# A conditioned residual kernel in fp32: new engine orders in its first two pairs, one copy and one split moved in every pair

## The chip, the cores and the metric

The kernel runs on one core of a Trainium2 chip. The metric is the device time of one execution in microseconds. Inside the core TensorE (PE) multiplies, VectorE (DVE), ScalarE (ACT) and GpSimd (POOL) work on whole tiles, and SyncE (SP) issues most DMAs. Each engine runs its own list of instructions in order and waits on semaphores that the others raise. PE has two clock levels, 1.2 and 2.4 GHz; the profile shows the granted clock as a share of the higher.

## The reference

```
B, C, T = 64, 128, 1024
w = cond_weights[conditions]                       # (64, 128, 128)
x = x + einsum('bct,bcd->bdt', x, w)               # residual 1, over channels
H = einsum('btd,od->bto', x, W)                    # W is 1024 x 1024
xa = einsum('btd,brd->btr', x, A[adapter])         # rank 16, 8 adapters
delta = einsum('btr,bor->bto', xa, Bm[adapter]) * scalings[adapter]
x = x + H + delta                                  # residual 2
```

The kernel swaps the two linear maps: it first multiplies the raw x by W plus identity (with the adapter columns riding along), and then by the batch's own 128 x 128 matrix plus identity.

## The kernel before, in words

The 64 batches are done in 32 pairs. The contraction over 1024 columns of x is cut into four blocks of 256, the 1024 columns of W into three of 342 (the last is shorter in truth), so a pair is 2 x 4 times a 4 x 3 grid of weight blocks, b00 to b32. From the second pair (pair 1) on, it isn't multiplied densely: 20 products of sums of x with sums of weight blocks (numbered 0 to 19, function `multiply`) give the two batches' results together. The sums of x (u, u12, u67, u910, u11, u54, u3) and the raw blocks (a001, a02, a03, a1, a13) are made for each pair, the 20 sums of weights once. Every operand is split in two halves of the fast fp32r type: ACT copies the high half (`hi_...`), DVE subtracts it to get the low half (`rest_...`), and PE does three matmuls, hi x hi, hi x lo, lo x hi. For the weights the same is done by `hi_of` and `rest_of`, and `in_place` is that for a sum that stands where its low half is kept.

Pair 0 has no split weights yet. PE multiplies it densely in full fp32 (`dense`, twelve blocks in the order of the table DENSE) while DVE and POOL make the sums of weights, each in the order of a table (DVE_SUMS, POOL_SUMS), and ACT and DVE split them (SPLITS). POOL adds the identity into blocks (`add_identity`, sums named i21a and so on) and scales the adapter's columns (`first_rides` for pair 0, `make_rides` and `rest_rides` for later ones).

After the products of a pair come its adapter part and its condition part. The xa columns are split on DVE (`split_xa`, `rest_xa`, batch 0 and batch 1 apart), PE turns them (`turn0`, `turn1`), ACT copies the turned ones to g_sb (`turned_xa`), and PE multiplies them with b_stack (`lora`), which holds the adapter's second factor in halves. It comes from b_split, a table in device memory that the kernel writes at its start from b_raw (halves made in z_hi and z_lo of batch 0). The results are split again (z_hi, z_lo) and multiplied by c_hi and c_lo (`condition`, into o_ps0 and o_ps1); ACT evacuates them into o_sb (`evacuate`), and SP stores o_sb, batch 1 first and then batch 0 through the same buffer, so that the evacuation of batch 0 waits for the store of batch 1 (semaphore stored).

`step(i, j)` on each engine is the list for one pair. `run_steps` loops over pairs 2 to 29 and then writes two more steps. Pairs 0 and 1 have lists written out by hand on ACT, DVE and PE, with the work of the weights among them; SP and POOL have their own starts. In the list of pair p on ACT and DVE stands also the making of x for pair p + 1. Waits are written by `after` (a semaphore counted in pairs) and `made` (a sum of weights). Lines of the trace are those of the helpers: L475 is every ACT copy, L826 every DVE subtraction and L829 every addition, L1089 DVE's sums of weights, L1260 a product, L1406 a dense block, L1275 `lora`, L1287 and L1280 the turns, L1296 to L1298 the condition product.

Of the kernel before, what the change touches and what calls it, by code (L numbers as in the profile page):

```python
# [4 lines left out]
P = 128  # L5
# [3 lines left out]
def cond_resid_kernel(nc, xT, cond_idx, adapter_idx, cond_w, wB, lora_a, lora_b, scalings, out):  # L9
    f32 = mybir.dt.float32  # L10
# [44 lines left out]
    DENSE = ("b12", "b01", "b30", "b21", "b20", "b10", "b00", "b11", "b31", "b02", "b32", "b22")  # L55
    SPLITS = ("17", "13", "15", "5", "2", "0", "4", "14", "18", "10", "7", "11", "9", "8", "16", "1", "3", "19", "6", "12")
    POOL_SUMS = ("i21a", "i21b", "i10", "i00", "i11a", "i11b", "i32", "i22")
    DVE_SUMS = ("s", "v", "5", "f", "2", "e", "0", "4", "14", "18", "y", "10", "7", "11a", "11", "9", "12a", "16a",
                "1a", "16", "6", "1", "3", "19a", "12", "19")

    with ExitStack() as ctx:
# [235 lines left out]

        @block.sync
        def _(sp):
# [41 lines left out]
            def load_w(b):  # L341
                k, j = int(b[1]), int(b[2])
                sp.dma_start(w_block(b), wB[k, j, :, :, :]).then_inc(w_landed[b], 16)  # L343

# [19 lines left out]

            load_x(0, 0, 0, 0)
            load_w("b12")
            load_x(0, 0, 0, 1)
            load_w("b01")
            load_w("b30")
            sp.dma_start(s_tab[:, :], scalings.to_broadcast([P, NAD])).then_inc(s_landed, 16)  # L370
            sp.wait_ge(adapter_landed, 16)
            load_a(0, 0, 0)
            load_w("b21")
            load_w("b20")
            sp.dma_start(b_raw[:, :], lora_b.rearrange("a r o -> (a r) o")).then_inc(b_raw_landed, 16)
            for b in ARRIVAL[5:]:
                load_w(b)
# [10 lines left out]
            sp.wait_ge(b_lo_ready, 1)  # L388
            for a in range(NAD):
                sp.dma_start(b_split[a, 1, :, :], z_lo[0][a * R:(a + 1) * R, :].bitcast(f32)).then_inc(b_saved, 16)  # L390
            sp.wait_ge(b_saved, 32 * NAD)
            load_b(0, 0, 0)
            step(0, 0)
            step(0, 1)
# [8 lines left out]
        def _(pool):  # L403
# [42 lines left out]
            pick_scalings(0, 0, 0)  # L446
            pool.wait_ge(a_landed, 32)
            pool.wait_ge(s_picked, 2)
            first_rides("b30")
            pool.wait_ge(w_landed["b21"], 16)  # L450
            add_identity("b21", 0, 170, 0, 128)
            add_identity("b21", 1, 298, 0, 44)
            first_rides("b20")
            first_rides("b10")
            first_rides("b00")
            pool.wait_ge(w_landed["b10"], 16)
# [3 lines left out]
            pool.wait_ge(w_landed["b11"], 16)  # L460
            add_identity("b11", 0, 0, 86, 42)
            add_identity("b11", 1, 42, 0, 128)
# [10 lines left out]
        def _(act):  # L473
# [121 lines left out]
            def hi_z00(i, j, d):  # L595
                after(act, lora_done["00"], i, j, d)
                after(act, o_done[0][0], i, j, d - 1)
                if exists(i, j, d) and not exists(i, j, d - 1):
                    act.wait_ge(b_saved, 32 * NAD)
                copy(z_hi[0][:, 0:N], main_of(bank_of(j, d, "alpha"))).then_inc(z_hi_ready["00"], 1)  # L600
# [43 lines left out]
            def step(i, j):  # L644
# [59 lines left out]

            act.dma_start(adapter_sb[:, :], adapter_idx).then_inc(adapter_landed, 16)
            act.wait_ge(ident_ready, 1)
# [4 lines left out]
            hi_of("13", slot("hi", "19"))  # L711
            made(act, "v")
            in_place("15")
            made(act, "5")
            in_place("5")
# [19 lines left out]
            hi_a02(0, 0, 1)  # L735
            dense_through(act, "b30", "b10", "b00", "b20")
            hi_rides(0, 0, 1)
            hi_u(0, 0, 1)
            hi_of_c(0, 0)
            hi_u910(0, 0, 1)  # L740
            turned_xa(0, 0, 0, 1)
            hi_u11(0, 0, 1)
            turned_xa(0, 0, 0, 0)
            made(act, "10")
            in_place("10")
            whole_block("10", c10_sb, "pi10")
            whole_block("11", c11_sb, "pi11")
            hi_z10(0, 0, 0)
            hi_z11(0, 0, 0)
            made(act, "7")  # L750
            in_place("7")
            made(act, "11", "e")
# [4 lines left out]
            made(act, "9", "f")  # L757
            in_place("9")
# [4 lines left out]
            whole_block("02", c02_sb, "pi02")  # L763
            begin_c10(0, 1)
            hi_z02(0, 1, -1)
            evacuate(0, 1, -1, 1, 0)
            hi_u54(0, 1, 0)
            seed_pi11(0, 1)
            evacuate(0, 1, -1, 1, 1)
            made(act, "10", "1a", "16a")  # L770
            in_place("8")
            begin_c11(0, 1)
            seed_pi10(0, 1)
            made(act, "6", "16")
# [22 lines left out]
            evacuate(0, 1, -1, 0, 1)  # L797
# [26 lines left out]
        def _(dve):  # L824
# [205 lines left out]
            def step(i, j):  # L1030
# [450 lines left out]
```

## Time and profile before

| | |
|---|---|
| timed runs | 807.81 us median of 3 (806.87 to 807.81) |
| the profiled execution | 805.12 us, of it a span of 803.2 us |
| PE busy | 768.1 us (96%) |
| DVE, ACT, POOL busy | 619.6, 510.9, 190.2 us |
| mean granted clock | 0.987 |

The span is what the trace shows from the first to the last instruction. From about 100 us on the trace repeats itself once a pair, and PE waits only once more, 2.2 us at the end. The first 100 us, in which the weights arrive and are summed and split, look different: in the 40 slices of the page PE has 6, 7, 8, 5, 7 tenths where it later has 9. A timeline row gives the start, the time of the row, the engine and line, the operation and its tiles, and in brackets how long the engine had been idle and what ended that.

### The profile page before, as it was taken

How to read it: one execution, taken by the hardware profiler on the slowest of the kernel's cores; microseconds unless marked ns; L12 is line 12 of the kernel's file. 1: busy time of each engine (PE TensorE's matmuls, PEld its weight loads, DVE VectorE, ACT ScalarE, POOL GpSimd, SP SyncE). 2: the span in 40 equal slices, each digit the busy share in tenths (PEclk: the TensorE clock that was granted, in tenths of full speed). 3: DMA queues.
4: the chain of work that ended last, by engine and by line, in shares of the span. 5: the costliest groups of instructions: out<-in, count | busy, mean ns of one | idle time of the engine just before them, and what ended most of it. 6: DMA issues, size and time to landing. Idle time of an engine off the chain costs nothing.

```text
span 803.2 us, 16853 instructions
## 1 busy us (share of the span) xinstructions
PE 768.1 (96%) x4456; PEld 728.4 (91%) x4456; DVE 619.6 (77%) x1397; ACT 510.9 (64%) x1186; POOL 190.2 (24%) x428
## 2 busy tenths in 40 slices
PE   6785799999999999999999999999999999999997
PEld 4464799999999999999999999999999999999996
DVE  5695977787887778788777878877787887777764
ACT  3364566667766666676666677666666766666663
POOL 4430221222222122222211222221122222112200
PEclk9998899999999999999999999999999999999999
DMA  8522134344323443432344343233434323343221
GB/s 294 145 93 86 59 120 138 129 132 144 102 101 120 134 137 124 144 108 97 122 131 144 118 144 115 95 123 125 142 118 144 126 90 125 119 140 118 86 87 78
DMA packets 47380, 98.26 MB, mean 122 GB/s; under 512 B 6788, under 2 KB 26244, under 8 KB 47364
## 3 DMA queue, kind: packets, MB, share of 16 engines
q1 hardware_dynamic: 47362, 98.08, 37.0%
q8 instruction: 6, 0.10, 0.1%
q14 instruction: 10, 0.08, 0.0%
q10 hardware_dynamic: 2, 0.00, 0.0%
HBM read 63.45 MB, written 34.60 MB: 122 GB/s over the span
## 4 chain that ended last, share of the span: by engine, by line
PE 87%; DVE 5%; SPq 3%; DMA 2%; issue 1%; ACT 1%; ACTq 0%; DVEq 0%
PE bank L1260 72%; PE o_ps L1296 4%; PE o_ps L1297 4%; PE o_ps L1298 3%; PE bank L1275 3%; DVE w_lo_raw L1089 1%; DVE w_lo L826 1%; SPq L343 1%; DMA cond_sb<-cond_idx 1%; DMA out<-o_sb 1%; DVE x_lo L826 1%; DVE z_lo L826 1%; SPq L387 0%; DVE c_sb L829 0%; PE bank L1280 0%
## 5 line engine op out<-in xcount | busy, mean ns | idle before, releaser
L1260 PE MATMUL bank<-w_hi,x_hi 128*128 128x342 f32 (+1 forms) x1240 | 404.4, 326 | 6.7 <-ACT c_sb L475 3.5
L1260 PE MATMUL bank<-w_lo,x_hi 128*128 128x342 f32 (+1 forms) x1240 | 400.8, 323 | 0.0
L1260 PE MATMUL bank<-w_hi,x_lo 128*128 128x342 f32 (+1 forms) x1240 | 400.5, 323 | 0.0
L1260 PEld LDWEIGHTS bank<-w_hi,x_hi 128*128 128x128 f32 x1240 | 234.5, 189 | 14.4 <-ACT c_sb L475 4.3
L1260 PEld LDWEIGHTS bank<-w_lo,x_hi 128*128 128x128 f32 x1240 | 234.1, 189 | 3.6
L1260 PEld LDWEIGHTS bank<-w_hi,x_lo 128*128 128x128 f32 x1240 | 234.6, 189 | 0.0
L826 DVE TENSOR_TENSOR x_lo<-x_raw,x_hi 128x256 fp32r<-128x256 f32 (+1 forms) x279 | 150.6, 548 | 34.7 <-ACT x_hi L475 29.4
L475 ACT ACTIVATE x_hi<-x_raw 128x256 fp32r<-128x256 f32 (+1 forms) x279 | 138.1, 507 | 57.2 <-PE bank L1260 51.0
L292 POOL TENSOR_TENSOR w_lo<-a_ride,w_hi 128x160 fp32r<-128x160 f32 x31 | 16.0, 518 | 539.6 <-ACT w_hi L475 539.6
L475 ACT ACTIVATE c_sb<-bank 128x342 f32<-128x342 f32 x190 | 85.4, 451 | 39.7 <-PE bank L1260 39.0
L475 ACT ACTIVATE o_sb<-o_ps 128x512 f32<-128x512 f32 x124 | 74.0, 597 | 36.6 <-PE o_ps L1298 26.2
L475 ACT ACTIVATE z_hi<-c_sb 128x340 fp32r<-128x340 f32 (+1 forms) x128 | 60.4, 490 | 54.5 <-DVE c_sb L829 54.5
L829 DVE TENSOR_TENSOR c_sb<-bank,c_sb 128x342 f32<-128x342 f32 x186 | 91.1, 504 | 3.8 <-PE bank L1275 2.6
L826 DVE TENSOR_TENSOR x_lo<-t_sb,x_hi 128x512 fp32r<-128x512 f32 x62 | 42.9, 691 | 41.0 <-ACT x_hi L475 41.0
L826 DVE TENSOR_TENSOR z_lo<-c_sb,z_hi 128x340 fp32r<-128x340 f32 (+1 forms) x128 | 69.2, 542 | 1.3 <-ACT z_hi L475 1.3
L1296 PE MATMUL o_ps<-z_hi,c_hi 128*128 128x512 f32 x126 | 53.3, 423 | 9.7 <-ACT g_sb L475 9.7
L826 DVE TENSOR_TENSOR xa_sum<-bank,c_sb 128x16 f32<-128x16 f32 x31 | 5.4, 174 | 65.3 <-PE bank L1260 65.3
L475 ACT ACTIVATE bank<-bank 128x342 f32<-128x342 f32 (+1 forms) x93 | 41.2, 443 | 15.8 <-PE bank L1260 15.8
L1297 PE MATMUL o_ps<-z_lo,c_hi 128*128 128x512 f32 x126 | 50.3, 399 | 0.0
L1298 PE MATMUL o_ps<-z_hi,c_lo 128*128 128x512 f32 x126 | 49.9, 396 | 0.0
L1275 PE MATMUL bank<-b_stack,g_sb 128*128 128x340 f32 (+1 forms) x192 | 45.9, 321 | 2.5 <-ACT g_sb L475 2.5
L268 POOL TENSOR_TENSOR a_ride<-a_now,s_now 128x32 f32<-128x32 f32 x93 | 43.3, 490 | 18.4 <-DMA a_now<-lora_a 11.7
(85 smaller groups left out, 846.9 us busy)
## 6 DMA issues: line engine op xcount, KB each, us to landing
x_raw<-xT SPq DMA_DIRECT2D x64, 512.0 KB, 4.6
out<-o_sb SPq DMA_DIRECT2D x62, 512.0 KB, 2.6
b_stack_raw<-b_split SPq DMA_DIRECT2D x128, 128.0 KB, 2.5
a_now<-lora_a SPq DMA_DIRECT2D x64, 64.0 KB, 3.3
c_raw<-cond_w SPq DMA_DIRECT2D x64, 64.0 KB, 1.8
w_lo_raw<-wB SPq DMA_DIRECT2D x7, 342.0 KB, 7.1
w_hi_raw<-wB SPq DMA_DIRECT2D x5, 342.0 KB, 6.4
out<-x_raw SPq DMA_DIRECT2D x4, 256.0 KB, 2.0
```

The lines of the kernel that those rows point to most:

```text
L268: unit.tensor_tensor(to, a_now[:, n, k:k + count, :], s_now[:, n:n + 1].unsqueeze(2).to_broadcast([P, count, 2 * R]), ALU.mult).then_inc(a ...
L292: unit.tensor_tensor(left_rides(w_lo), rides(0, 5), left_rides(w_hi), ALU.subtract).then_inc(ride_ready, 1)
L343: sp.dma_start(w_block(b), wB[k, j, :, :, :]).then_inc(w_landed[b], 16)
L475: return nc.scalar.activation(to, x, ACT.Copy)
L826: return nc.vector.tensor_tensor(to, x, y, ALU.subtract)
L829: return nc.vector.tensor_tensor(to, x, y, ALU.add)
L1089: nc.vector.tensor_tensor(to, x, y, op).then_inc(dve_summed, 1)
L1260: last = nc.tensor.matmul(bank[:, lo:hi], x[:, left, c * C:(c + 1) * C], w[:, c, FIRST[o]:FIRST[o] + WIDTH[o]], start=opens and c == 0 and ...
L1275: nc.tensor.matmul(main_of(bank_of(j, d, role), cols.stop - cols.start), g_sb[n][:, :], b_stack[:, cols], start=False, stop=True, skip_gro ...
L1296: nc.tensor.matmul(bank[:, :], c_hi[:, n, :], z_hi[n][:, cols], start=True, stop=False)
L1297: nc.tensor.matmul(bank[:, :], c_hi[:, n, :], z_lo[n][:, cols], start=False, stop=False)
L1298: nc.tensor.matmul(bank[:, :], c_lo[:, n, :], z_hi[n][:, cols], start=False, stop=True)\
```

## The change

Pair 0 and pair 1 get other lists; two things also change in `step`, which all later pairs run.

- In `step` of ACT the copy of batch 1's turned columns (`turned_xa(i, j, 0, 1)`) goes ahead of the evacuation of batch 0's first half. In `step` of DVE the split of batch 0's columns and its rest stand next to each other and ahead of the u11 rest.
- SP's start: b12 comes first; b01 and the scalings are issued from ACT's queue; b11 comes ahead of b_raw. b_split is written by two DMAs of 512 KB instead of sixteen of 64 KB, and they stand ahead of the small loads of adapters and conditions.
- SP's list of pair 1: the two stores of pair 0's outputs come first, pair 3's x after them.
- POOL adds the identity to b21 before it scales columns, and to b11 before b10 and b00.
- PE takes the dense b21 before b30, and both turns only after the dense b31 and b02; b32 goes ahead of the first `lora`.
- ACT and DVE have other hand-written orders in pair 0 and pair 1 (ACT takes b_stack much later in pair 0; DVE makes e, 18 and y earlier).

```
@@ step of ACT
                 begin_c02(i, j)
+                turned_xa(i, j, 0, 1)
                 if exists(i, j, -1):
                     evacuate(i, j, -1, 0, 0)
-                turned_xa(i, j, 0, 1)
@@ step of DVE
                 sum_c11(i, j)
+                split_xa0(i, j)
                 if exists(i, j, 1):
                     rest_u11(i, j, 1)
-                split_xa0(i, j)
+                rest_xa0(i, j)
                 rest_z("10", i, j, 0)
-                rest_xa0(i, j)
@@ SP, its start and pair 1
+            def save_b(part, z):
+                sp.dma_start(b_split[:, part, :, :], z[:, :].bitcast(f32)).then_inc(b_saved, 16)
+            load_w(sp, "b12")
             load_x(0, 0, 0, 0)
-            load_w("b12")
             load_x(0, 0, 0, 1)
-            load_w("b01")
...
+            sp.wait_ge(b_hi_ready, 1)
+            save_b(0, z_hi[0])
+            sp.wait_ge(b_lo_ready, 1)
+            save_b(1, z_lo[0])
             sp.wait_ge(first_scaled, 8)
             load_a(0, 0, 1)
             sp.wait_ge(cond_landed, 16)
             load_c(0, 0, 0)
-            sp.wait_ge(b_hi_ready, 1)
-            for a in range(NAD):
-                sp.dma_start(b_split[a, 0, :, :], z_hi[0][a * R:(a + 1) * R, :].bitcast(f32)).then_inc(b_saved, 16)
...
             step(0, 0)
-            step(0, 1)
+            load_b(0, 1, 0)
+            store(0, 1, -1, 1)
+            load_a(0, 1, 2)
+            store(0, 1, -1, 0)
+            after(sp, lo_ready["u54"], 0, 1, 0)
...
+            load_x(0, 1, 2, 0)
+            load_x(0, 1, 2, 1)
+            load_c(0, 1, 1)
@@ PE, pair 0
             dense("b12")
             dense("b01")
+            made(pe, "i21b")
+            dense("b21")
             pe.wait_ge(first_scaled, 2)
             dense("b30")
...
+            dense("b31")
+            dense("b02")
             pe.wait_ge(ident_r_ready, 1)
             turn1(0, 0)
             turn0(0, 0)
-            dense("b31")
-            dense("b02")
+            made(pe, "i32")
+            dense("b32")
@@ ACT, pair 0
             in_place("18")
+            hi_a001(0, 0, 1)
+            hi_a03(0, 0, 1)
             hi_u12(0, 0, 1)
-            hi_a001(0, 0, 1)
-            take_b(0, 0)
-            hi_a03(0, 0, 1)
...
             hi_u11(0, 0, 1)
-            turned_xa(0, 0, 0, 0)
+            take_b(0, 0)
             made(act, "10")
             in_place("10")
+            turned_xa(0, 0, 0, 1)
+            turned_xa(0, 0, 0, 0)
@@ DVE, pair 0
             rest_of("17", w_block("b12"))
             add("s", slot("hi", "19"), w_block("b12"), w_block("b01"), ALU.subtract)
+            rest_of("13", slot("hi", "19"))
             dve.wait_ge(w_landed["b30"], 16)
```

ACT in pair 0, from the copies of x for pair 1 to the first adapter results. b_stack is the adapter's second factor, a_ride the scaled adapter columns, g_sb the turned columns. Before:

```order
L475 ACTIVATE x_hi<-t_sb 128x512
L475 ACTIVATE x_hi<-x_raw1 128x512
L475 ACTIVATE b_stack<-b_stack_raw 128x1024
L475 ACTIVATE x_hi<-x_raw1 128x256
L475 ACTIVATE x_hi<-x_raw1 128x512
L475 ACTIVATE x_hi<-x_raw1 128x256
L475 ACTIVATE w_hi<-a_ride 128x5x2x16
L475 ACTIVATE w_hi<-a_ride 128x4x2x16
L475 ACTIVATE x_hi<-u_sb 128x256
```

And now:

```order
L484 ACTIVATE x_hi<-u_sb 128x256
L484 ACTIVATE w_hi<-a_ride 128x5x2x16
L484 ACTIVATE w_hi<-a_ride 128x4x2x16
L484 ACTIVATE c_hi<-c_raw 128x256
L484 ACTIVATE x_hi<-t_sb 128x512
L484 ACTIVATE x_hi<-x_raw1 128x256
L484 ACTIVATE b_stack<-b_stack_raw 128x1024
L484 ACTIVATE w_hi<-w_lo_raw 128x2x342
L484 ACTIVATE g_sb1<-o_ps1 128x128
```

The copy of b_stack has moved from ahead of six copies (three of x, two of the rides, one of u) to behind all of them and those of c, u910 and u11 too.

SP in the list of pair 1, before, behind the loads into b_stack_raw (x_raw1 is the buffer of the odd pairs, out<-o_sb a store):

```order
L323 DMA b_stack_raw<-b_split 32x1024 x2
L303 DMA x_raw1<-xT 128x1024 x2
L339 DMA out<-o_sb 128x1024
L308 TENSOR_LOAD adapter_sb
L308 ISA x2
```

And now:

```order
L327 DMA b_stack_raw<-b_split 32x1024 x2
L343 DMA out<-o_sb 128x1024
L312 TENSOR_LOAD adapter_sb
L312 ISA x2
...
L318 DMA a_now<-lora_a 128x128
L343 DMA out<-o_sb 128x1024
L307 DMA x_raw1<-xT 128x1024 x2
```

The first store has moved ahead of the loads of x, and the loads of x behind both stores.

ACT in pair 1, around the copy of batch 1's turned columns, before:

```order
L475 ACTIVATE o_sb<-o_ps0 128x512
L475 ACTIVATE g_sb1<-o_ps1 128x128
L475 ACTIVATE w_hi<-w_lo_raw 128x2x342 x3
L475 ACTIVATE x_hi<-t_sb 128x512
L475 ACTIVATE o_sb<-o_ps1 128x512
```

And now:

```order
L484 ACTIVATE o_sb<-o_ps0 128x512
L484 ACTIVATE g_sb1<-o_ps1 128x128
L484 ACTIVATE o_sb<-o_ps1 128x512
L484 ACTIVATE w_hi<-w_lo_raw 128x2x342 x3
L484 ACTIVATE x_hi<-t_sb 128x512
```

The evacuation of o_ps1 has moved ahead of the last three weight splits (19, 6, 12) and a copy of x.

## Rows read from the trace of the kernel before

**Rows 1.** Windows: stretch, its length, busy time by engine, clock, DMA share, GB/s.

```profile
100.00:123.36 23.36, 23.36 (x142) 22.60 (x141) 18.11 (x43) 15.30 (x37) 5.31 (x13) 1.00 0.37 125
```

**Rows 2.** Waits of PE in the first 100 us: total, times, longest.

```profile
PE o_ps L1296 <- ACT g_sb L475: 9.7, 1, 9.7
```

**Rows 3.** Waits of DVE in the first 100 us, the small early ones.

```profile
DVE w_lo_raw L1089 <- POOL w_lo_raw L429: 1.2, 1, 1.2
...
DVE w_hi_raw L1089 <- POOL w_hi_raw L429: 0.7, 1, 0.7
DVE w_hi_raw L1089 <- DMA w_hi_raw<-wB: 0.5, 1, 0.5
DVE z_lo L826 <- ACT z_hi L475: 0.4, 1, 0.4
```

**Rows 4.** Timeline of DVE, its start and the instructions behind its long waits.

```profile
7.66 0.87 DVE L826 TENSOR_TENSOR w_lo<-w_lo_raw,w_hi 128x684 fp32r<-128x684 f32 x1 [5.89 <-ACT w_hi L475]
...
40.76 0.52 DVE L826 TENSOR_TENSOR x_lo<-u_sb,x_hi 128x256 fp32r<-128x256 f32 x1 [7.28 <-ACT x_hi L475]
...
78.93 0.87 DVE L826 TENSOR_TENSOR w_lo<-w_lo_raw,w_hi 128x684 fp32r<-128x684 f32 x1 [8.03 <-ACT w_hi L475]
...
88.25 0.43 DVE L826 TENSOR_TENSOR x_lo<-x_raw,x_hi 128x256 fp32r<-128x256 f32 x1 [0.74 <-ACT x_hi L475]
```

**Rows 5.** Timeline of PE: turn, two dense blocks, product 17 twice, one slow matmul.

```profile
32.57 0.44 PE L1287 MATMUL o_ps<-ident_r,xa_cols 128*128 128x128 f32 x1 [3.92 <-DVE xa_cols L826]
...
33.02 6.29 PE L1406 MATMUL bank<-w_lo_raw,x_raw 128*128 128x342 f32 x16
...
48.38 0.58 PE L1260 MATMUL bank<-w_hi,x_hi 128*128 128x342 f32 x1
...
80.33 0.50 PE L1260 MATMUL bank<-w_hi,x_lo 128*128 128x358 f32 x1
...
88.74 0.42 PE L1260 MATMUL bank<-w_hi,x_hi 128*128 128x342 f32 x1 [1.64 <-DVE x_lo L826]
```

**Rows 6.** Timeline of ACT: b_raw, b_stack, the evacuation of pair 0, three weight splits.

```profile
14.91 1.06 ACT L475 ACTIVATE z_hi<-b_raw 128x1024 fp32r<-128x1024 f32 x1 [2.49 <-DMA b_raw<-lora_b]
...
37.81 1.06 ACT L475 ACTIVATE b_stack<-b_stack_raw 128x1024 fp32r<-128x1024 f32 x1 [8.51 <-DMA b_stack_raw<-b_split]
...
77.47 0.60 ACT L475 ACTIVATE o_sb<-o_ps 128x512 f32<-128x512 f32 x1 [10.35 <-DMA out<-o_sb]
...
78.12 2.10 ACT L475 ACTIVATE w_hi<-w_lo_raw 128x684 fp32r<-128x684 f32 x3
```

**Rows 7.** Timeline of SP's queue: saves, loads from b_split, the first store.

```profile
23.01 3.67 SPq L387 DMA_DIRECT2D b_split<-z_hi  x8
26.72 3.65 SPq L390 DMA_DIRECT2D b_split<-z_lo  x8
33.64 1.77 SPq L323 DMA_DIRECT2D b_stack_raw<-b_split  x4
...
71.30 0.38 SPq L339 DMA_DIRECT2D out<-o_sb  x1
```

**Rows 8.** Windows while large loads and while small saves run, columns as in rows 1.

```profile
18.00:20.00 2.00, 2.00 (x8) 1.27 (x8) 1.79 (x3) 0.91 (x2) 2.00 (x3) 1.00 1.08 381
...
26.00:28.00 2.00, 2.00 (x9) 1.30 (x8) 2.00 (x3) 0.77 (x1) 1.92 (x3) 1.00 0.73 135
```

**Rows 9.** Timeline of POOL, the first and the last row of pair 1's rides.

```profile
24.46 2.18 POOL L268 TENSOR_TENSOR a_ride<-a_now,s_now 128x32 f32<-128x32 f32 x3 [0.31 <-DMA a_now<-lora_a]
...
29.98 0.31 POOL L288 TENSOR_TENSOR a_ride<-a_now,a_ride 128x32 f32<-128x32 f32 x1
```

**Rows 10.** Timeline of a steady pair: ACT's g_sb copy, DVE's u11 rest, product 17.

```profile
133.74 0.27 ACT L475 ACTIVATE g_sb<-o_ps 128x128 fp32r<-128x128 f32 x1
...
137.97 0.42 DVE L826 TENSOR_TENSOR x_lo<-x_raw,x_hi 128x256 fp32r<-128x256 f32 x1
...
140.28 0.32 PE L1260 MATMUL bank<-w_hi,x_hi 128*128 128x342 f32 x1
```

More of the change, by code:

```diff
@@ L53, in cond_resid_kernel @@
     ARRIVAL = ("b12", "b01", "b30", "b21", "b20", "b11", "b10", "b00", "b32", "b31", "b02", "b22")
[L55 to L58, printed above, removed]
+    DENSE = ("b12", "b01", "b21", "b30", "b20", "b10", "b00", "b11", "b31", "b02", "b32", "b22")
+    SPLITS = ("17", "13", "5", "15", "2", "0", "4", "14", "18", "10", "7", "11", "9", "8", "16", "1", "3", "19", "6", "12")
+    POOL_SUMS = ("i21a", "i21b", "i11a", "i11b", "i10", "i00", "i32", "i22")
+    DVE_SUMS = ("s", "5", "v", "f", "e", "2", "0", "18", "4", "y", "14", "10", "7", "11a", "11", "12a", "9", "16a",
                 "1a", "16", "6", "1", "3", "19a", "12", "19")
@@ L363, in step @@
                     load_c(i, j, 1)
+            def save_b(part, z):
+                sp.dma_start(b_split[:, part, :, :], z[:, :].bitcast(f32)).then_inc(b_saved, 16)
+            load_w(sp, "b12")
             load_x(0, 0, 0, 0)
-            load_w("b12")
             load_x(0, 0, 0, 1)
-            load_w("b01")
-            load_w("b30")
-            sp.dma_start(s_tab[:, :], scalings.to_broadcast([P, NAD])).then_inc(s_landed, 16)
+            load_w(sp, "b30")
+            load_w(sp, "b21")
             sp.wait_ge(adapter_landed, 16)
             load_a(0, 0, 0)
-            load_w("b21")
-            load_w("b20")
+            load_w(sp, "b20")
+            load_w(sp, "b11")
             sp.dma_start(b_raw[:, :], lora_b.rearrange("a r o -> (a r) o")).then_inc(b_raw_landed, 16)
-            for b in ARRIVAL[5:]:
-                load_w(b)
+            for b in ARRIVAL[6:]:
+                load_w(sp, b)
             sp.dma_start(cond_sb[:, :], cond_idx).then_inc(cond_landed, 16)
@@ L384, in _ @@
             load_c(0, 0, 0)
-            sp.wait_ge(b_hi_ready, 1)
-            for a in range(NAD):
-                sp.dma_start(b_split[a, 0, :, :], z_hi[0][a * R:(a + 1) * R, :].bitcast(f32)).then_inc(b_saved, 16)
[L388 to L391, printed above, removed]
+            sp.wait_ge(b_saved, 32)
             load_b(0, 0, 0)
             step(0, 0)
-            step(0, 1)
+            load_b(0, 1, 0)
[3 more added lines that the diff above has]
+            after(sp, lo_ready["u54"], 0, 1, 0)
+            after(sp, lo_ready["a02"], 0, 1, 0)
+            after(sp, lo_ready["u3"], 0, 1, 0)
+            load_x(0, 1, 2, 0)
+            load_x(0, 1, 2, 1)
+            load_c(0, 1, 1)
             run_steps(sp, step)
@@ L446, in _ @@
             pick_scalings(0, 0, 0)
+            pool.wait_ge(w_landed["b21"], 16)
+            add_identity("b21", 0, 170, 0, 128)
+            add_identity("b21", 1, 298, 0, 44)
             pool.wait_ge(a_landed, 32)
@@ L455, in _ @@
             first_rides("b00")
+            pool.wait_ge(w_landed["b11"], 16)
+            add_identity("b11", 0, 0, 86, 42)
+            add_identity("b11", 1, 42, 0, 128)
             pool.wait_ge(w_landed["b10"], 16)
@@ L703, in in_place @@
                 hi_of(o, slot("lo", o))
+            load_w(act, "b01")
             act.dma_start(adapter_sb[:, :], adapter_idx).then_inc(adapter_landed, 16)
+            act.dma_start(s_tab[:, :], scalings.to_broadcast([P, NAD])).then_inc(s_landed, 16)
             act.wait_ge(ident_ready, 1)
@@ L711, in _ @@
             hi_of("13", slot("hi", "19"))
+            made(act, "5")
+            in_place("5")
             made(act, "v")
             in_place("15")
-            made(act, "5")
-            in_place("5")
             act.wait_ge(b_raw_landed, 16)
@@ L1145, in _ @@
             first_rest(0)
+            add_identity_c(0, 0)
             sum_u910(0, 0, 1)
[L1147 removed]
             rest_u(0, 0, 1)
             sum_u11(0, 0, 1)
+            rest_c(0, 0)
             rest_u910(0, 0, 1)
[L1151 removed]
             rest_u11(0, 0, 1)
[L1153 to L1155 removed]
             made(dve, "y")
             add("10", slot("lo", "10"), slot("hi", "6"), slot("lo", "8"), ALU.subtract)
+            in_place("18")
             rest_u67(0, 0, 1)
@@ L1222, in _ @@
             rest_xa0(0, 1)
+            sum_u67(0, 1, 1)
+            rest_u12(0, 1, 1)
             sum_u910(0, 1, 1)
@@ L1413, in _ @@
             dense("b01")
+            made(pe, "i21b")
+            dense("b21")
             pe.wait_ge(first_scaled, 2)
             dense("b30")
-            made(pe, "i21b")
-            dense("b21")
-            pe.wait_ge(first_scaled, 8)
+            pe.wait_ge(first_scaled, 4)
             dense("b20")
+            pe.wait_ge(first_scaled, 6)
             made(pe, "i10")
             dense("b10")
+            pe.wait_ge(first_scaled, 8)
             made(pe, "i00")
@@ L1435, in _ @@
             lora("12", 0, 0, 0)
-            made(pe, "i32")
-            dense("b32")
             made(pe, "i22")
```

100 lines of the change are left out of this document (44 added, 56 removed).

## The prediction, made before the changed kernel ran

> **What bounds the kernel now.** I first took the windows. Once the pairs run at their regular pace, PE is busy for the whole of its window: 23.36 us of 23.36 at clock 1.00, beside 18.11 on DVE and 15.30 on ACT [rows 1]. Orders on ACT or DVE can gain nothing there. What there is to win lies in the first 100 us, so I read the waits of that stretch. PE stood still 9.7 us for a copy into g_sb [rows 2]. DVE has four small waits of 1.2, 0.7, 0.5 and 0.4, together 2.8 us [rows 3], and three that its timeline shows.
>
> Which engine carries the first 90 us? Take the single stalls of DVE: it starts at 7.66, stands 7.28 us before 40.76, runs without a break from there until 70.90, stands 8.03 us before 78.93, and 0.74 us before 88.25 [rows 4]. That last instruction makes the low half of u11, and PE's product 17 of pair 2 waits for it and starts at 88.74 [rows 5]. So the first 88.74 us are the work of DVE plus its stalls, and PE has room in them. From product 17 of pair 2 on, order and work are nearly the same in both kernels and soon PE is full. The gain is therefore what is taken off DVE's ledger up to that product.
>
> The causes of the two large stalls are on other engines. At 37.81 ACT has stood 8.51 us for b_stack_raw, with the copies that DVE needs (u, u910, c) queued behind it; at 77.47 it has stood 10.35 us for an output store, with the weight splits 19, 6 and 12 behind it [rows 6]. The first goes back to SP: sixteen 64 KB saves of b_split, issued from 23.01 to 30.37, and only then the loads from it at 33.64. The second: the store of pair 0's batch 1 is issued at 71.30, since SP first waits for the low half of a02 and issues pair 3's x; ACT goes on 6.2 us later [rows 6, 7].
>
> **The change part by part.** I keep DVE's ledger, with the durations of the trace.
>
> (1) Start. b12 now goes first and b01 beside it from ACT's queue. Before, x of batch 0 (512 KB) and b12 (342 KB) were ahead of DVE's first split. Now it is b12 with up to 342 KB of b01: 170 to 512 KB less, at 381 GB/s [rows 8] 0.45 to 1.35 us earlier. I take the middle, **+0.9**. PE pays for it: x of batch 0 is behind 342 KB more, so PE starts 0.9 us later. That is free, since PE has slack until the pair 1 products. The row shows the DMA engines at a share of 1.08, with no capacity to spare. The Trainium skill ("DMA: Bandwidth & Descriptors", section "Issuing engines are not separate DMA queues") says that DMAs started from different engines run on the same 16 engines and interleave, and that a second queue saves only issue time; by that the term is 0.45, and the total 0.45 less. It speaks against this part, not against the rest.
>
> (2) Early waits. The old four small ones, 2.8 us, go or are replaced. New: the split of 13 stands directly behind the sum s and has to wait for ACT's copy of s, 0.1 plus 0.78, say 0.9. b_raw is now behind b11 too (342 KB more); ACT got it at 14.91 [rows 6], now at about 15.85; with 1.06 for the copy, z_lo can start at 16.9. DVE, with seven 684-element instructions at 0.78 to 0.9 more behind it, gets there at about 15.7: 1.2. The sum f has its identity block earlier, since POOL does b21 first. b30 has as many bytes ahead of it as before, so about 0.1. Net **+2.8 - 2.2 = +0.6**.
>
> (3) The stall of 7.28. Two saves of 512 KB replace sixteen issues (7.36 us of SP's queue), and they go ahead of the adapter loads. ACT now takes b_stack after all the copies for pair 1. But the saves lie in the queue behind x of pair 1 and ahead of the small loads. All loads end near 24.0 (3.5 MB after b_raw's 14.9 at about 385 GB/s); 1.05 MB of saves at 381 GB/s takes 2.7 us more, so b_split is saved and a_now is there at about 27. POOL's rides take from 24.46 to 30.29, 5.83 us [rows 9], so now they end at 32.9. ACT copies their high halves (0.5) and those of c (0.3) before the u910 copy; DVE gets to the rest of c at about 33.4, finds it ready at 33.75, and has to wait for u910 once more. I put 0.7 on this new wait. The loads from b_split are issued at 28.7 and land at about 33, ahead of the copy of b_stack that ACT reaches at 34.6, and PE wants the lora products at 37. Net **+7.28 - 0.7 = +6.6**. Its ends: a wait of 0 (+7.3), and the saves at the 135 GB/s of the old ones, 7.8 us instead of 2.7, which puts 5.1 us more on the rides (+1.5). I take the high rate, because the slow one belongs to a queue with a 64 KB issue every 0.46 us. The Trainium skill's same page ("Anatomy of one DMA") has about 2 us plus bytes over 436 GB/s for a DMA (a fit of another issue path), and so 3.2 us for one of 512 KB; by that a save would be down before x is, the wait would be 0 and the total 0.7 more. The old chain, one small transfer after another at 135 GB/s, agrees that issue and not bytes held it.
>
> (4) The turns on PE move behind two dense blocks, 16 matmuls that took 6.29 us partly at the lower clock [rows 5] (4.8 at the higher). The 3.92 us of PE's wait ahead of the turns is gone, and it costs nothing: DVE's columns are ready at 31, the turns come at 34.7. PE gets to product 17 of pair 1 at about 40 instead of 48.4, DVE is 8.1 earlier there, so the two stay in step. A new stop on PE: ACT's u54 copy and three others stand ahead of the seed of pi11, which makes product 0 wait 1 to 2 us. DVE doesn't hang on it.
>
> (5) The stall of 8.03. SP now issues the store when both halves of batch 1 are out, near 49.7, and even with the 6.2 us of the old one it lands at 56; ACT wants the buffer at about 59. The evacuation and the copy to g_sb run at once, and PE's second condition product isn't held. What is late next: the split of 19 needs ACT's copy, now behind the evacuation of the second half. PE's turn ends near 59.4, product 16 takes six steps of 0.16 [rows 10], 0.95; the condition product, of wider matmuls, 0.7; the evacuation 0.6 and the split 0.77 or less [rows 6]: 62.4. DVE arrives at 63.2. So **+8.0**, with 0.8 us to spare. Pair 3's x and pair 2's c are issued later now (x near 62), but they are first needed past 80.
>
> (6) Orders of the steady pairs. ACT copies g_sb before an evacuation; DVE's two short column instructions come together, ahead of the u11 rest. ACT: the g_sb copy is 0.27 long, and the evacuation slips by about 0.35 [rows 10]. DVE: the u11 rest of 0.42, started at 137.97, slips by up to 0.33, and product 17 starts at 140.28: 1.9 us of cover. **0**. At the tail PE waits on neither.
>
> Sum: 0.9 + 0.6 + 6.6 + 8.0 = **16.1 us**. Against the profiled execution: 805.12 - 16.1 = 789.0, span 803.2 - 16.1 = 787.1. The three timed runs have a median of 807.81, 2.7 above the profiled one; I carry the gain over to them: 807.81 - 16.1 = **791.7 us**.
>
> **Rivals.** *The small loads pile up behind the saves.* The saves run at the old 135 GB/s and the rides end 5.1 us later. For it: there is 1 MB in front of them that wasn't there. Against: the engines moved 381 GB/s as long as they had large transfers [rows 8]. Gain 16.1 - 5.1 = 11.0: **796.8**.
>
> *PE falls to its lower clock in pair 1.* With DVE the bound, PE gets several short stops from 58 to 73 (about 0.7, 0.9, 0.6, 1.5, 3). At 1.2 GHz a matmul takes 0.50 instead of 0.32 [rows 5, 10], and one starts every 0.30 instead of 0.16. The nine between the turn and the split of 19 and what hangs on them then take 1.4 more, of which 0.8 is spare; with a longer low stretch in pair 2 I put 2 us on it: **793.7**.
>
> *Fewer new waits.* The 2.2 and 0.7 don't come, and the start gives its upper end of 0.45 more: gain 19.5, **788.3**.
>
> *The steady orders cost every pair.* If the 0.35 on ACT and 0.33 on DVE weren't covered, each of 29 pairs would grow by 0.68: 19.7 us, more than the gain, 807.8 - 16.1 + 19.7 = **811.4**, slower than before. It decides from 0.56 us a pair (16.1 / 29). Against it: the 1.9 us of cover.
>
> *The store isn't early.* If it were held by the loads ahead of it on SP and landed after 59 + 8, the second stall would stay: **799.7**. Against it: nothing that it waits for ends after 50.
>
> **How the numbers follow.** Forecast 0.60; lower clock 0.15; pile-up 0.10; fewer waits 0.07; store not early 0.03; no gain by some collision unseen 0.02; steady cost 0.03. The range reaches from just above the case of fewest waits to just past the pile-up: 789.0 to 797.5. The measurement tells 0.2% (1.6 us) from no change. Faster 0.95, same 0.02, slower 0.03.
>
> **What would show it.** On DVE: no stall of over 2 us between 20 and 60, and none of 8 near 62; the low half of u11 at about 72. On ACT: no wait for b_stack_raw over 1 us and none for the store. On SP: the store issued near 50, before pair 3's x. On PE: product 17 of pair 1 near 40, of pair 2 near 72.6; waits in pair 1 that point at DVE; windows of 23.36 us as before. It is wrong if the small waits of DVE before 35 sum to over 4 us, if the copy of 19 is behind DVE, or if a steady window grows.

## The result, and the profile after

| | before | after |
|---|---|---|
| timed runs, median | 807.79 us of 4 (806.87 to 807.81) | 783.69 us of 4 (783.24 to 784.22) |
| ratio | | 0.9705, 95% interval 0.9688 to 0.9721 |
| the profiled execution | 805.12, span 803.2 | 783.24, span 781.3 |
| mean clock | 0.987 | 0.993 |

The change takes 24.1 us off, or 21.9 in the spans of the two profiled executions. I had said 16.1 and a range of 789.0 to 797.5: the sign was right, the size was too small, and the time lies outside the range.

The part that I had worked out came as forecast. The timeline of DVE in the kernel after, with its start and what answers to [rows 4] (the same columns):

```profile
6.53 0.87 DVE L837 TENSOR_TENSOR w_lo<-w_lo_raw,w_hi 128x684 fp32r<-128x684 f32 x1 [4.76 <-ACT w_hi L484]
...
9.03 0.87 DVE L837 TENSOR_TENSOR w_lo<-w_hi_raw,w_hi 128x684 fp32r<-128x684 f32 x1 [0.84 <-ACT w_hi L484]
...
33.95 0.53 DVE L837 TENSOR_TENSOR c_lo<-c_raw,c_hi 128x256 fp32r<-128x256 f32 x1 [0.36 <-ACT c_hi L484]
...
62.99 0.86 DVE L837 TENSOR_TENSOR w_lo<-w_lo_raw,w_hi 128x684 fp32r<-128x684 f32 x1
...
72.06 0.43 DVE L837 TENSOR_TENSOR x_lo<-x_raw,x_hi 128x256 fp32r<-128x256 f32 x1 [0.74 <-ACT x_hi L484]
```

DVE starts 1.13 us earlier than at 7.66, both long stalls are gone (the split of 19 at 62.99 waits for nothing), and the low half of u11 starts at 72.06 instead of 88.25. The causes on the other engines, to be held beside [rows 6, 7], SP's queue first and then ACT:

```profile
15.99 0.73 SPq L366 DMA_DIRECT2D b_split<-z_hi  x1
17.48 0.64 SPq L366 DMA_DIRECT2D b_split<-z_lo  x1
...
29.14 1.80 SPq L327 DMA_DIRECT2D b_stack_raw<-b_split  x4
...
49.35 0.37 SPq L343 DMA_DIRECT2D out<-o_sb  x1
```

```profile
34.65 1.04 ACT L484 ACTIVATE b_stack<-b_stack_raw 128x1024 fp32r<-128x1024 f32 x1
...
58.82 0.59 ACT L484 ACTIVATE o_sb<-o_ps 128x512 f32<-128x512 f32 x1
```

ACT waits neither for b_stack_raw nor for the store any more: neither row has a bracket. And PE (timeline), the first dense block, then product 17 of pair 1 and of pair 2:

```profile
7.48 4.90 PE L1418 MATMUL bank<-w_lo_raw,x_raw 128*128 128x342 f32 x8 [7.48 <-DMA x_raw<-xT]
...
40.08 0.58 PE L1272 MATMUL bank<-w_hi,x_hi 128*128 128x342 f32 x1
...
72.54 0.65 PE L1272 MATMUL bank<-w_hi,x_hi 128*128 128x342 f32 x1 [3.24 <-DVE x_lo L837]
```

Product 17 of pair 2 starts at 72.54; before it was 88.74 [rows 5]. That is 16.2 us, against 16.1 forecast. That the two agree so well is partly luck. Here are the windows up to the low half of u11, before and then after. Behind the length a line has the busy time and the number of instructions of PE, of its weight loads, of DVE, ACT and POOL, and at its end clock, DMA share and GB/s; DVE's is the third pair.

```profile
0.00:88.25 88.25, 61.88 (x241) 46.72 (x241) 62.14 (x105) 39.79 (x77) 25.97 (x49) 0.90 0.47 146
```

```profile
0.00:72.06 72.06, 56.50 (x241) 42.54 (x241) 62.74 (x105) 39.60 (x77) 28.49 (x49) 0.99 0.52 179
```

DVE runs 105 instructions up to there in both kernels. Its idle time fell from 26.1 to 9.3 us, 16.8 less, and the same number of instructions took 0.6 us longer, which my ledger had left out. Also, the traces scatter here: in four that share the old lists of pairs 0 and 1 product 17 of pair 2 starts at 88.61 to 89.46, in two that share the new ones at 72.54 and 73.18. A hit to 0.1 is finer than that.

The other 5.7 us of the span must come after product 17 of pair 2, where I had put zero. They do. The chain of work that ended last has one long piece of ten products in each pair (start, length, what). Here are the first and the last of these pieces past 100 us, in the kernel before and then in the kernel after:

```profile
122.74 9.70 PE bank L1260 x60
...
776.67 9.68 PE bank L1260 x60
```

```profile
105.87 9.69 PE bank L1272 x60
...
754.43 9.68 PE bank L1272 x60
```

There are 29 of these pieces in either, so 28 periods from the first to the last: 653.93 / 28 = 23.355 us a pair before, 648.56 / 28 = 23.163 after. A steady pair has become 0.192 us shorter; 29 of them are 5.6 us. Together 16.2 + 5.6 = 21.8 of the 21.9. Two small terms cancel in this: between product 17 of pair 2 and the first long piece (99.35 before, 82.70 after) the lead grows by 0.45 us, and behind the last one it shrinks by 0.3. Neither was looked into.

Where does PE lose 0.19 us in a pair in which it is busy 100% of the time and no wait is counted? It shows in the steps from the start of one matmul to the start of the next. The timeline of PE before, from the end of product 16 to the condition product of batch 0's second half:

```profile
133.71 0.32 PE L1260 MATMUL bank<-w_lo,x_hi 128*128 128x342 f32 x1
133.86 0.32 PE L1260 MATMUL bank<-w_hi,x_lo 128*128 128x342 f32 x1
134.07 0.50 PE L1296 MATMUL o_ps<-z_hi,c_hi 128*128 128x512 f32 x1
134.40 0.40 PE L1297 MATMUL o_ps<-z_lo,c_hi 128*128 128x512 f32 x1
```

And the same place after:

```profile
116.84 0.32 PE L1272 MATMUL bank<-w_lo,x_hi 128*128 128x342 f32 x1
117.00 0.32 PE L1272 MATMUL bank<-w_hi,x_lo 128*128 128x342 f32 x1
117.16 0.40 PE L1308 MATMUL o_ps<-z_hi,c_hi 128*128 128x512 f32 x1
117.39 0.40 PE L1309 MATMUL o_ps<-z_lo,c_hi 128*128 128x512 f32 x1
```

Before, the condition product starts 0.21 after its neighbour where 0.16 is the rule, is 0.50 long instead of 0.40, and its successor starts 0.33 later instead of 0.23: 0.05 + 0.10. Past 100 us the row is this long (0.50 or 0.51, in the last two pairs 0.46) once in each of the 30 pairs, and never in the kernel after. The ACT row of [rows 10] suggests why: the copy into g_sb started at 133.74 and took 0.27, so it ended at 134.01, just as PE wanted to go on at about 134.02. In the program PE waits for that copy ahead of this product, because the product overwrites the tile that is copied.

The last 0.05 is at the turn of batch 0:

```profile
139.17 0.27 PE L1280 MATMUL bank<-ident_r,xa_cols 128*128 128x128 f32 x1
139.28 0.37 PE L1260 MATMUL bank<-w_hi,x_hi 128*128 128x342 f32 x1
```

Its successor starts 0.11 later; in the kernel after the step is 0.06 (122.18 to 122.24). DVE's rest of the columns, which the turn needs, ended at 139.00, 0.17 ahead of the turn; in the kernel after it ended 0.62 ahead. Neither delay counts as a wait in the profile, since rows of PE overlap each other. That these are waits is so far an inference; the first experiments test it.

### The profile page after: what moved, and what is told of

It reads as the page before. It is cut to its first block, busy times and chain, and to the rows that moved or that the text cites. A ratio compares the mean times of both kernels' runs of the same rounds, so it can differ in the third digit from the quotient of the medians.

```text
span 781.3 us, 16842 instructions
## 1 busy us (share of the span) xinstructions
PE 758.3 (97%) x4456; PEld 724.7 (93%) x4456; DVE 620.7 (79%) x1397; ACT 509.2 (65%) x1186; POOL 191.7 (25%) x428
## 4 chain that ended last, share of the span: by engine, by line
PE 88%; DVE 6%; POOL 2%; DMA 2%; issue 1%; ACT 1%; SPq 0%; ACTq 0%; POOLq 0%; DVEq 0%
PE bank L1272 74%; PE o_ps L1309 4%; PE bank L1287 4%; PE o_ps L1308 4%; PE o_ps L1310 4%; DVE w_lo_raw L1100 1%; DVE w_lo L837 1%; DVE x_lo L837 1%; DMA s_tab<-scalings 1%; DMA a_now<-lora_a 1%; POOL w_hi_raw L432 1%; DVE z_lo L837 1%; DVE c_sb L840 0%; POOL w_lo_raw L432 0%; DVE x_raw L837 0%
## 5 line engine op out<-in xcount | busy, mean ns | idle before, releaser
L292 POOL TENSOR_TENSOR w_lo<-a_ride,w_hi 128x160 fp32r<-128x160 f32 x31 | 16.2, 522 | 516.5 <-ACT w_hi L484 516.5
L1308 PE MATMUL o_ps<-z_hi,c_hi 128*128 128x512 f32 x126 | 49.6, 393 | 0.0
```

The source lines that it names most:

```text
L292: unit.tensor_tensor(left_rides(w_lo), rides(0, 5), left_rides(w_hi), ALU.subtract).then_inc(ride_ready, 1)
L1308: nc.tensor.matmul(bank[:, :], c_hi[:, n, :], z_hi[n][:, cols], start=True, stop=False)
```

## The experiments

All comparisons are with the kernel before, timed beside each kernel on the same chip, with ratios and 95% intervals. Its medians there were 806.07, 806.39 and 807.37 us. The kernel after wasn't timed again beside them; where I compare with it, I take its ratio of 0.9705. One per cent is 8.06 us. A ratio isn't formed from the two medians, and can differ from their quotient by up to 0.1%.

### The two moves in the steps, alone and together

ACT's move alone, in the kernel before:

```
                 begin_c02(i, j)
+                turned_xa(i, j, 0, 1)
                 if exists(i, j, -1):
                     evacuate(i, j, -1, 0, 0)
-                turned_xa(i, j, 0, 1)
```

> The kernel before, with one change: in ACT's step the copy of batch 1's turned columns stands ahead of the evacuation. Theory H (hidden waits): in a steady pair of the kernel before the condition product starts 0.05 us late and its second matmul 0.10 us late, though the profile counts no wait, because the copy into g_sb ends at the moment PE needs it. The move takes about 0.14 us off each of 29 pairs: 4.1 us, period 23.21 instead of 23.36. Rival N (my prediction): nothing in steady pairs, 0.0 us.

DVE's move alone:

```
                 sum_c11(i, j)
+                split_xa0(i, j)
                 if exists(i, j, 1):
                     rest_u11(i, j, 1)
-                split_xa0(i, j)
+                rest_xa0(i, j)
                 rest_z("10", i, j, 0)
-                rest_xa0(i, j)
```

> The kernel before, with one change: in DVE's step the split of batch 0's columns is closed up ahead of the u11 rest. Theory H: the turn of batch 0 on PE is held 0.05 us in a pair, so 29 x 0.05 = 1.5 us, period 23.31. Rival N: 0.0.

Both moves, still with the old lists of pairs 0 and 1:

> The kernel before, with both moves in the steps. Theory H: they add up, 0.19 us a pair, 5.6 us, period 23.17. A rival in which one wait hides the other: the larger alone, about 4 us. Rival N: 0.0.

And the kernel after with the two steps set back:

> The changed kernel with the two steps as before: only the lists of pairs 0 and 1 and SP's and POOL's starts are new. Theory H: 5.6 us of the gain go, the time is about 18.5 us under the kernel before (the 16.2 by which product 17 of pair 2 came earlier, and 2 that nobody has explained yet), period 23.36. Rival: the gain was made all in the first pairs and stays near 24.

| kernel | median us | ratio (95%) | period of a steady pair |
|---|---|---|---|
| ACT's move | 803.08 | 0.9953 (0.9940 to 0.9966) | 23.213 |
| DVE's move | 804.21 | 0.9972 (0.9960 to 0.9984) | 23.298 |
| both moves | 801.28 | 0.9934 (0.9921 to 0.9946) | 23.164 |
| after, steps set back | 789.29 | 0.9783 (0.9769 to 0.9797) | 23.350 |

The periods come from the chains of the four, read as above. In the same order, with 30, 30, 29 and 29 pieces:

```profile
101.51 9.70 PE bank L1260 x60
...
774.68 9.68 PE bank L1260 x60
```

```profile
100.19 9.70 PE bank L1260 x60
...
775.83 9.68 PE bank L1260 x60
```

```profile
122.49 9.67 PE bank L1260 x60
...
771.08 9.68 PE bank L1260 x60
```

```profile
107.47 9.68 PE bank L1272 x60
...
761.26 9.68 PE bank L1272 x60
```

ACT's move gives 0.142 a pair, DVE's 0.057, both together 0.191: they add up, as the hidden waits want it, and no interval holds 1. The spans of single traces are too coarse for this: with ACT's move alone the span is only 1.9 us shorter, since that trace is already 2.2 us behind at its first long piece (101.51 against 99.35). With the steps set back the period is the old one to 0.005 us, and 17.5 us of gain remain (806.07 x 0.0217; 16.8 between the medians). The two places can be told apart. With DVE's move alone the condition product still starts late, and the turn doesn't (PE's timeline of that kernel):

```profile
134.61 0.32 PE L1260 MATMUL bank<-w_hi,x_lo 128*128 128x342 f32 x1
134.82 0.50 PE L1296 MATMUL o_ps<-z_hi,c_hi 128*128 128x512 f32 x1
135.15 0.40 PE L1297 MATMUL o_ps<-z_lo,c_hi 128*128 128x512 f32 x1
...
139.92 0.22 PE L1280 MATMUL bank<-ident_r,xa_cols 128*128 128x128 f32 x1
139.98 0.37 PE L1260 MATMUL bank<-w_hi,x_hi 128*128 128x342 f32 x1
```

The steps from 134.61 to 134.82 and to 135.15 are the slow ones of before, the step from the turn to its successor is 0.06. With ACT's move alone the condition product is on time in every pair past 101 us, and the step behind the turn is still 0.08 to 0.09. So the cause of the 0.19 us is shown, each part by its own move. My prediction, nothing in steady pairs, is refuted.

### The store

The kernel before with only SP's list of pair 1 changed:

```
             step(0, 0)
-            step(0, 1)
+            load_b(0, 1, 0)
+            store(0, 1, -1, 1)
+            load_a(0, 1, 2)
+            store(0, 1, -1, 0)
+            after(sp, lo_ready["u54"], 0, 1, 0)
+            after(sp, lo_ready["a02"], 0, 1, 0)
+            after(sp, lo_ready["u3"], 0, 1, 0)
+            load_x(0, 1, 2, 0)
+            load_x(0, 1, 2, 1)
+            load_c(0, 1, 1)
```

> The kernel before with one change: SP's list of pair 1 issues both stores of pair 0 ahead of pair 3's x. My reason (the store holds the evacuation, behind it g_sb and three weight splits): the 8.03 us stall of DVE and the 9.7 of PE go, 7 to 8 us less. Rival (DVE or ACT has another wait right behind): under 4 us.

The same edit undone in the kernel after:

> The changed kernel with SP's old list of pair 1 (pair 3's x before the stores). My reason: the store is issued near 63 and lands near 69, ACT's split of 19 and with it DVE is 8 to 9 us late: 8 to 9 us more than the changed kernel. Rival: ACT's new order of pair 1 hides half of it, 4 us.

The first came to 797.11 us, ratio 0.9887 (0.9868 to 0.9907): 9.1 us less, in its profile 7.9 (span 795.3). The second came to 793.92, ratio 0.9852 (0.9831 to 0.9873). By the ratios that is 1.47% or 11.8 us more than the kernel after, by the medians 10.2, in its profile 9.9 (span 791.2); I had expected 8 to 9. Its timelines of SP, ACT, DVE and PE show the old stall again:

```profile
62.22 0.83 SPq L307 DMA_DIRECT2D x_raw<-xT  x2
63.14 0.38 SPq L343 DMA_DIRECT2D out<-o_sb  x1
```

```profile
69.30 0.60 ACT L475 ACTIVATE o_sb<-o_ps 128x512 f32<-128x512 f32 x1 [10.40 <-DMA out<-o_sb]
...
71.80 0.60 ACT L475 ACTIVATE o_sb<-o_ps 128x512 f32<-128x512 f32 x1 [1.74 <-PE o_ps L1301]
72.30 2.09 ACT L475 ACTIVATE w_hi<-w_lo_raw 128x684 fp32r<-128x684 f32 x3
```

```profile
73.10 0.87 DVE L828 TENSOR_TENSOR w_lo<-w_lo_raw,w_hi 128x684 fp32r<-128x684 f32 x1 [9.93 <-ACT w_hi L475]
```

```profile
70.12 0.79 PE L1299 MATMUL o_ps<-z_hi,c_hi 128*128 128x512 f32 x1 [9.71 <-ACT g_sb L475]
...
82.66 0.66 PE L1263 MATMUL bank<-w_hi,x_hi 128*128 128x342 f32 x1 [3.23 <-DVE x_lo L828]
```

The store goes out behind x at 63.14 and ACT goes on 6.2 us later, as in the kernel before. Product 17 of pair 2 starts at 82.66 instead of 72.54. The reason holds, and in the new lists it is worth more than the 8.0 of my sum: DVE stands 9.93 us. In ACT's new list of pair 1 the evacuation of the second half stands ahead of the three weight splits, and it has to wait 1.74 us for PE's condition product. So the splits start 3.0 us behind the evacuation of 69.30, where they started 0.65 behind it before [rows 6].

### b_stack: the saves and the place of its copy

Sixteen saves in the old place, in the kernel after (number and place change together, so this run doesn't separate them):

```
-            sp.wait_ge(b_hi_ready, 1)
-            save_b(0, z_hi[0])
-            sp.wait_ge(b_lo_ready, 1)
-            save_b(1, z_lo[0])
             sp.wait_ge(first_scaled, 8)
...
             load_c(0, 0, 0)
-            sp.wait_ge(b_saved, 32)
+            sp.wait_ge(b_hi_ready, 1)
+            for a in range(NAD):
+                sp.dma_start(b_split[a, 0, :, :], z_hi[0][a * R:(a + 1) * R, :].bitcast(f32)).then_inc(b_saved, 16)
...
+            sp.wait_ge(b_saved, 32 * NAD)
```

> The changed kernel, with b_split saved by sixteen small DMAs behind the small loads, as before. Issue takes 7.3 us, the loads from b_split land near 41 instead of 33, ACT takes b_stack 6 us later. In the changed order only the splits of 10 and what follows hang behind it: 2 to 4 us more. Rival (the place of b_stack on ACT was the whole cause and the saves are hidden): within 0.5 us.

The copy of b_stack back ahead of the copies of x:

```
             in_place("18")
+            take_b(0, 0)
             hi_a001(0, 0, 1)
...
             hi_u11(0, 0, 1)
-            take_b(0, 0)
```

> The changed kernel with the copy of b_stack on ACT back ahead of the copies of x for pair 1. It waits there for the load until about 33.4, and the low half of u12 on DVE, now at 30.2, comes near 36.5: 5 to 6.5 us more. Rival (the new place is of no weight once the saves are two DMAs): under 1 us.

And both at once:

> The changed kernel with both: sixteen saves in the old place and the copy of b_stack ahead of the copies of x. Alone they cost 3.1 and 4.7 us. If the two are one chain (the copy waits for the saves), together they cost more than their sum, about 11, since everything for pair 1 then hangs on a landing near 41. If they are separate causes: 7.8.

| kernel | median us | ratio (95%) | product 17 of pair 2 at |
|---|---|---|---|
| after | 783.69 | 0.9705 (0.9688 to 0.9721) | 72.54 |
| old saves | 786.78 | 0.9756 (0.9737 to 0.9776) | 75.67 |
| copy early | 788.40 | 0.9782 (0.9762 to 0.9801) | 77.64 |
| both | 793.90 | 0.9834 (0.9819 to 0.9850) | 83.22 |

In the traces, up to product 17 of pair 2, they cost 3.1, 5.1 and 10.7 us; between the medians of the timed runs it is 3.1, 4.7 and 10.2. The last is more than the sum of 8.2 or 7.8: it is one chain, and each edit cuts it in another place. ACT's timeline with the saves old, with the copy early, and with both:

```profile
39.54 1.06 ACT L486 ACTIVATE b_stack<-b_stack_raw 128x1024 fp32r<-128x1024 f32 x1 [4.76 <-DMA b_stack_raw<-b_split]
```

```profile
33.45 1.06 ACT L484 ACTIVATE b_stack<-b_stack_raw 128x1024 fp32r<-128x1024 f32 x1 [5.27 <-DMA b_stack_raw<-b_split]
```

```profile
39.12 1.06 ACT L486 ACTIVATE b_stack<-b_stack_raw 128x1024 fp32r<-128x1024 f32 x1 [11.10 <-DMA b_stack_raw<-b_split]
```

With both, DVE stands 10.94 us for ACT's half of u12. The data is there near 39 with the sixteen saves and near 33 with the two; what hangs behind the copy decides what that costs.

The costs of undoing single parts don't share out the gain: the store undone (10.1 us at product 17) and both b_stack edits undone (10.7) already make more than 16.2. POOL's order, the order of the dense blocks and the other new orders of ACT and DVE were never run alone.

### The start, the turns, and one order more

b01 and the scalings back on SP's queue:

```
-            load_w(act, "b01")
             act.dma_start(adapter_sb[:, :], adapter_idx).then_inc(adapter_landed, 16)
-            act.dma_start(s_tab[:, :], scalings.to_broadcast([P, NAD])).then_inc(s_landed, 16)
...
             load_x(0, 0, 0, 1)
+            load_w(sp, "b01")
             load_w(sp, "b30")
+            sp.dma_start(s_tab[:, :], scalings.to_broadcast([P, NAD])).then_inc(s_landed, 16)
```

> The changed kernel, with b01 and the scalings issued from SP (behind x of pair 0) instead of ACT's queue. b01 lands near 9 instead of 7.3, so the sum s and the split of 13 come 1.5 us later; the wait for b30 behind them (0.4) and the 0.5 at 21 take up part: 0.5 to 1.2 us more than the changed kernel. Rival (DMAs of two queues share the same engines, nothing is won): 0.0 to 0.2.

784.78 us, ratio 0.9726 (0.9710 to 0.9741), product 17 of pair 2 at 73.29: 0.75 us later in the trace. The timed ratio is 0.2% above that of the kernel after, and the two intervals overlap, so the timed runs don't tell the two kernels apart. DVE's timeline:

```profile
5.12 0.87 DVE L837 TENSOR_TENSOR w_lo<-w_lo_raw,w_hi 128x684 fp32r<-128x684 f32 x1 [3.35 <-ACT w_hi L486]
8.73 0.87 DVE L1100 TENSOR_TENSOR w_hi_raw<-w_lo_raw,w_hi_raw 128x684 f32<-128x684 f32 x1 [2.73 <-DMA w_hi_raw<-wB]
```

b12 alone at the head lets DVE start at 5.12, 1.4 us before the kernel after; but then the sum s waits for b01 until 8.73, where the kernel after had it at 7.32. What counts is when both are there. The additions that start at 21.27 in the kernel after, and between 21.15 and 21.35 in seven other traces with its start, start at 22.20 here: up to that point 0.9 us are lost beyond the scatter. That 0.75 of it is still there at product 17 isn't shown, since there the traces scatter by as much.

The turns on PE back ahead of the dense b31 and b02:

```
             dense("b11")
-            dense("b31")
-            dense("b02")
             pe.wait_ge(ident_r_ready, 1)
             turn1(0, 0)
             turn0(0, 0)
+            dense("b31")
+            dense("b02")
```

> The changed kernel with the two turns on PE ahead of the dense b31 and b02 as before. PE waits near 29 for DVE's columns (ready at 31.9), 2.9 us, and is that much later at the first adapter product. My step (4): DVE carries the stretch and has the room, 0 to 0.5 us. Rival: PE's 2.9 us go through c10 and c11 to DVE's z halves, 1 to 3 us.

784.24 us, ratio 0.9719 (0.9705 to 0.9734), product 17 of pair 2 at 73.03, 0.5 us later. Neither the timed runs nor the trace tell this from nothing: the kernel after with its steps set back, whose lists up to there are the same, has 73.18. Against the rival's 1 to 3 us speak the trace and the medians (0.55 apart), its upper part at least.

The u11 chain of pair 1 first, on DVE and ACT:

```
             sum_u910(0, 1, 1)
-            add_identity_c(0, 1)
             sum_u11(0, 1, 1)
-            sum_c11(0, 1)
             rest_u(0, 1, 1)
+            add_identity_c(0, 1)
             rest_u11(0, 1, 1)
+            sum_c11(0, 1)
...
+            hi_u11(0, 1, 1)
             hi_of_c(0, 1)
             hi_u910(0, 1, 1)
             hi_a001(0, 1, 1)
-            hi_u11(0, 1, 1)
```

> The changed kernel, in pair 1 the u11 chain ahead of c: DVE makes sum u11 and the u rest before the identity of c, ACT copies u11 before c, u910 and a001. Product 17 of pair 2 then starts near 71.1 instead of 72.5. If this product's operand is the last thing that holds PE: 1 to 1.4 us less. Rival (rides, u910 and the z halves on DVE are next and unchanged): 0 to 0.4 us less.

783.26 us, ratio 0.9701 (0.9687 to 0.9715): not told apart from the kernel after. PE's timeline says where the head start went:

```profile
71.94 0.40 PE L1272 MATMUL bank<-w_hi,x_hi 128*128 128x342 f32 x1 [2.69 <-DVE c_sb L840]
76.13 0.67 PE L1272 MATMUL bank<-w_hi,x_hi 128*128 128x358 f32 x1 [2.25 <-POOL w_lo L293]
```

Product 17 starts 0.6 us earlier, now held by DVE's c11 (I had expected 71.1, it is 71.94), and product 5 then waits 2.25 us for POOL's rides and starts at 76.13, where the kernel after has it at 75.78. The rival was right: product 17's operand isn't the only thing that holds PE there.

## Why the prediction was right and wrong, step by step

**What bounds the kernel.** Right for the first 90 us: DVE's ledger gave product 17 of pair 2 at 72.6, and it came at 72.54. The mechanism is right, the closeness is luck: the stalls shrank by 16.8, not 16.1, DVE's instructions took 0.6 us more, and equal lists scatter by 0.6 to 0.9 us at this point.

**The step that failed** is (6), "Orders of the steady pairs", and the sentence ahead of it, that orders on ACT or DVE can gain nothing where PE is busy 23.36 of 23.36 us. I took a busy share of 100% and a list of waits with nothing in it for proof that PE never waited. I asked what the two moves could cost and never whether they gave anything. The runs put 0.142 us a pair on ACT's move and 0.057 on DVE's, 5.6 us over the run, and this alone puts the time below my range: 791.7 - 5.6 = 786.1.

**The base of the sum** is the other part, 786.1 against 783.69. I carried the gain over from the profiled execution of the kernel before (805.12) to the median of its timed runs (807.81), 2.7 us above. On the profiled execution the same sum gives 805.12 - 16.1 - 5.6 = 783.4, and the kernel after took 783.24 there; its timed median lies only 0.45 above that. So 2.2 us of the miss come from a distance that the kernel after doesn't have. 807.81 was also near the top of what the kernel before does: later its timed runs lay between 804.7 and 808.1, and against its later medians (806.07 to 807.37) the gain is 22.4 to 23.7, not 24.1. Why single executions of it spread like this stays open. The steady pairs of its trace don't show it: apart from the last two the periods are 23.32 to 23.39 before and 23.14 to 23.19 after.

**(1) and (2), start and early waits: sizes in part off.** The start came at +1.13 for 0.9, and not at the 0.45 that the prediction sets beside it; over the traces DVE starts at 7.09 to 7.87 with the old order and at 6.18 to 6.59 with the new one. I had b_raw too late: ACT got it at 14.90, not 15.85, and z_lo had no wait. Instead the wait for b30 was 0.39 and the one ahead of 21.27 0.52. The split of 13 waited 0.84 for the 0.9 that I had. With a wait of 0.24 at 26.68 the new waits sum to 2.0 for my 2.2.

**(3), the stall of 7.28: right.** a_now was there later than I thought (POOL started at 28.38, not 27), but POOL's chain took 4.6 us for 5.8, and the two errors cancelled; c's rest waited 0.36 and ACT took b_stack at 34.65 without waiting, for my 34.6. That the two edits form one chain is shown by the run with both.

**(4), the turns: right.** Product 17 of pair 1 came at 40.08. The place of the turns, put back, gave 0.5 us in one trace, which isn't told from nothing; that fits a move that costs and gives nothing on DVE's path.

**(5), the store: right in its reason**, and 7.9 us alone on the kernel before for the 8.0. What the order on SP is worth depends on the other lists, though: undone in the kernel after it costs 9.9.

**The rivals.** The saves didn't pile up: both were issued by 18.1 and the loads behind them went out at 29.14, 0.4 later than I had it. PE did fall to its lower clock (granted 0.50), but not in pair 1: from 70.6 to 77.4, beginning 1.3 us into the stop of 3.24 us ahead of product 17 of pair 2. The shorter stops before it, 0.53, 0.70, 0.39 and 1.13 us, left the clock at 1.00. In the kernel before it was low four times in the first 100 us (about 33 to 36, 43 to 46, 73 to 84 and 94 to 97). What this is worth after product 17 of pair 2 was not separated. The steady cost, my case for a slower kernel, was looked for on the right lines and with the wrong sign.

## What to carry to other kernels

A busy share of 100% doesn't say that nothing waits: where matmul rows overlap, look at the step from start to start, and compare each place with its neighbours. An operand that is ready only just before it is wanted is a suspect (here a copy that ended 0.01 us and columns that ended 0.17 us ahead; with 0.5 and 0.6 us nothing was lost), and a loss of 0.2 us in a loop of 30 turns is worth as much as a stall of 6 us that leaps to the eye. In a stretch bound by one engine, a ledger of that engine's stalls, with what each new order puts in their place, forecast a start 72 us into the kernel to a tenth of a microsecond, but several of its terms were off by up to 1 us and cancelled, and equal lists scatter by more than that tenth: the ledger finds what to change, and its last digit is luck. And a gain read from one profiled execution goes on that execution, with the spread of the timed runs named beside it.

## What the runs showed of the hardware that I hadn't expected

- A wait of PE that is shorter than the overlap of its rows shows as a longer row: 0.50 instead of 0.40 for the 128x512 matmul whose output tile wasn't released in time, with the following one 0.10 late, once in each of 30 pairs of the kernel before, and no more once ACT's copy came earlier.
- A load issued from ACT's queue beside SP's b12 landed by 7.32 where from SP, behind 1 MB of x, it landed at 8.73, and b12 itself came 1.4 us later for it. The Trainium skill ("DMA: Bandwidth & Descriptors", section "Issuing engines are not separate DMA queues") says that they interleave on the same engines; this trace agrees, and what the second queue changed was the order, worth 0.9 us of DVE's time up to 22 us.
- Sixteen saves of 64 KB were replaced by two of 512 KB, issued from 15.99 on instead of from 24.55 (kernel after with the old saves), and the data that is read back from them was in place near 33 instead of near 39 us. Number and place changed together; no run separates them.
